# A Mamba block with an FP4-quantised feed-forward: the two silu visits of a chunk each split into two halves

## What is computed

```python
h = layernorm(x) * (1 + ca) + sa
xc, z = split(h @ W_in.T)                 # 1024 channels each
xc = silu(causal_conv(xc))                # four taps per channel
dlt, B, C = split(xc @ W_xproj.T)         # 32, 16, 16 columns
delta = softplus(dlt @ W_dt.T + b_dt)
# for each channel d and each of 16 states n, over time t:
s[t] = exp(delta * A)[t] * s[t-1] + (delta * B * xc)[t]
y[t] = sum_n s[t, d, n] * C[t, n] + D * xc
x = x + ga * ((y * silu(z)) @ W_out.T)
x = x + gb * ffn(layernorm(x) * (1 + cb) + sb)   # three fp4-quantised linears
```

## Time and profile before

| | |
|---|---|
| median of 3 runs | 5216.49 us (5215.18 to 5220.55) |
| the profiled execution | 5215.41 us, span 5213.5 us |
| mean granted TensorE clock | 0.979 of full speed |
| busy share of the span | PE 91%, DVE 91%, POOL 73%, ACT 66% |
| first scan to first scan of the next chunk | 214.9 to 215.4 us in the chunks after the first |

### The profile page before, as it was taken

The page is one execution under the profiler, slowest core; times in us unless marked ns, Lnnn a source line. Parts: engine busy times, 40 slices in busy tenths (PEclk is TensorE's granted clock), DMA queues, the critical chain, the costliest instruction groups (busy, mean ns, idle before and its releaser), DMA issues. The chain is left out here.

```text
span 5213.5 us, 65887 instructions
## 1 busy us (share of the span) xinstructions
PE 4746.8 (91%) x21964; PEld 3282.5 (63%) x21964; DVE 4731.3 (91%) x3781; ACT 3466.9 (66%) x7501; POOL 3807.4 (73%) x1770
## 2 busy tenths in 40 slices
PE   8789899898988988989889898877999999999999
PEld 3455555555555555555555555555888888888888
DVE  7899999999999999999999999997888888888887
ACT  3787878778787787877877778765444444444442
...
GB/s 252 173 188 191 190 198 184 195 191 187 201 183 193 195 186 201 182 192 196 187 203 184 192 193 182 192 174 156 25 33 35 31 31 37 31 31 37 31 31 29
DMA packets 402664, 745.70 MB, mean 143 GB/s; under 512 B 44083, under 2 KB 44211, under 8 KB 402198
## 3 DMA queue, kind: packets, MB, share of 16 engines
...
...
## 5 line engine op out<-in xcount | busy, mean ns | idle before, releaser
L725 POOL TENSOR_TENSOR slot<-du,b_row 128x1024 f32<-128x1024 f32 x1024 | 2395.7, 2367 | 2.2 <-DMA down_quantised<-slot 1.2
L1070 DVE TENSOR_TENSOR_SCAN decays<-decays,state,slot 128x1024 f32<-128x1024 f32 x704 | 1650.2, 2344 | 43.8 <-ACT slot L944 42.7
L935 ACT ACTIVATE decays<-delta,rate 128x512 f32<-128x512 f32 x2048 | 1328.5, 681 | 24.4 <-issue 0.2
L1203 PEld LDWEIGHTS y_ps<-ident,slot 128*128 128x128 f32 x8192 | 957.6, 144 | 307.0 <-issue 246.2
L1126 PE MATMUL work_ps<-h_t,win 128*128 128x512 f32 x2048 | 958.5, 612 | 158.1 <-ACT delta L859 109.1
L1203 PE MATMUL y_ps<-ident,slot 128*128 128x128 f32 x8192 | 1039.0, 277 | 38.6 <-POOL slot L732 26.9
L1076 DVE TENSOR_TENSOR slot<-decays,c_row 128x1024 f32<-128x1024 f32 x704 | 861.7, 1224 | 68.6 <-DVE decays L1070 2.3
L1588 POOL TENSOR_TENSOR hq<-hid,qinv 128x1408 f32<-128x1408 f32 x63 | 163.4, 2593 | 1018.5 <-DVE qinv L1614 1018.5
L732 POOL TENSOR_TENSOR slot<-slot,c_row 128x1024 f32<-128x1024 f32 x320 | 755.1, 2360 | 147.6 <-ACT state L921 145.6
L1070 DVE TENSOR_TENSOR_SCAN slot<-decays,state,slot 128x1024 f32<-128x1024 f32 x320 | 749.9, 2343 | 47.1 <-ACT slot L944 47.1
L1126 PEld LDWEIGHTS work_ps<-h_t,win 128*128 128x128 f32 x2048 | 382.0, 195 | 586.2 <-issue 468.0
...
## 6 DMA issues: line engine op xcount, KB each, us to landing
b_row<-b_c_rows SPq DMA_DIRECT2D x1024, 256.0 KB, 3.9
c_row<-b_c_rows SPq DMA_DIRECT2D x1024, 256.0 KB, 3.7
...
```

Source lines behind the costliest of these rows:

```text
L725: pool.tensor_tensor(slot[:, u % SLOTS, :, :], du[:, p % 2, :, :], two(b_row[:, u % BC_RING, :]), ALU.mult).then_inc(S["ub_ready"], 1)
L935: act.activation(decay[u % 2][:, i, :], delta[:, p % 2, i, :], ACT.Exp, scale=rate[:, 2 * p + i, n:n + 1]).then_inc(S["decay_ready"], 1)
L1070: dve.tensor_tensor_scan(d if u in DVE_C else h, d, h, state[:, 2 * p, n:n + 1], ALU.mult, ALU.add).then_inc(S["scan_done"], 1)
L1203: op = pe.matmul(y_ps[i][:, s, :], slot[:, u % SLOTS, i, s * P:(s + 1) * P], ident[:, :], is_transpose=True, start=False, stop=(n == N - 1 ...
```

## The change

Each silu piece gets an argument h of 0 or 1 and works on four channel blocks (128 x 2048), with a table load before and after it as the whole one had. `silu_z` stands in units 11 and 21, `silu_x` in units 45 and 53. The semaphores of the two count two per chunk: a gate of blocks 0 to 3 waits for the first half alone; `x`, `du` and `xd` wait for both halves of xc.

All tables are written anew. Unit 8 and unit 19 are now in `DVE_C` and unit 9 is not; unit 48 takes the place of unit 47. So 45 units instead of 44 have their product with C on DVE. Four of the 49 bank numbers differ. The core of the diff:

```diff
 BANK = {
-    ("c", 7): 1, ("i", 1): 0, ("o", 2): 1, ("y", 3): 0,
+    ("c", 7): 0, ("i", 1): 1, ("o", 2): 0, ("y", 3): 1,
...
 ACT_STEPS = {
-    20: [("residual", 2, -1)], 21: [("silu_z", 0, 0)],
-    53: [("silu_x", 0, 1)], 54: [("z_out", 0, 1)],
+    10: [("z_out", 6, 0), ("residual", 0, -1)], 11: [("silu_z", 0, 0)],
+    20: [("residual", 2, -1), ("ln_apply", 2, 1), ("y_out", 1, 0)],
+    21: [("silu_z", 1, 0)], 22: [("ln_apply", 3, 1)],
+    45: [("in_out", 6, 1), ("silu_x", 0, 1)], 53: [("silu_x", 1, 1)],
...
 DVE_STEPS = {
-    (4, 0): [("gate", 6, -1)], (4, 1): [("gate", 7, -1)], (21, 0): [("gate", 0, 0)], (52, 1): [("gate", 5, 0)],
+    (4, 1): [("gate", 6, -1), ("gate", 7, -1)], (20, 1): [("gate", 0, 0)], (52, 0): [("gate", 5, 0)],
...
-                    def silu_z(_, c):
-                        for ka in last_pieces("z").values():
-                            wait(act, *piece_read(*ka, c))
-                        act.activation(zs[:, :, :], zs[:, :, :], ACT.Silu).then_inc(S["zs_ready"], 1)
+                    def silu_z(h, c):
+                        part = range(h * NB // 2, (h + 1) * NB // 2)
+                        for j in {BANK["z", j]: j for j in part}.values():
+                            wait(act, *piece_read("z", j, c))
+                        v = zs[:, part.start:part.stop, :]
+                        act.activation(v, v, ACT.Silu).then_inc(S["zs_ready"], 1)
                         act.preload_act_table_set("natural_log_exp_and_others")
...
-                        wait(dve, S["zs_ready"], c.at(1, 1))
+                        wait(dve, S["zs_ready"], c.at(2, j // (NB // 2) + 1))
...
-                        wait(pe, S["xc_ready"], c.at(1, 1))
+                        wait(pe, S["xc_ready"], c.at(2, 2))
```

More of the change, by code:

```diff
@@ L60 @@
[L60 to L64, removed]
@@ L65 @@
-    34: [("conv_out", 1, 1), ("y_out", 3, 0), ("y_out", 2, 0), ("xd", 4, 0)], 36: [("in_out", 3, 1)],
-    37: [("conv_out", 2, 1), ("xd", 7, 0)], 38: [("in_out", 4, 1)], 39: [("softplus", 3, 0)],
-    41: [("conv_out", 3, 1), ("xd", 6, 0)], 43: [("conv_out", 4, 1)], 44: [("lead", 3, 0), ("in_out", 5, 1)],
-    45: [("in_out", 6, 1)], 46: [("conv_out", 5, 1)], 48: [("conv_out", 6, 1)], 49: [("in_out", 7, 1)],
-    50: [("conv_out", 7, 1)], 51: [("y_out", 5, 0), ("y_out", 4, 0)], 53: [("silu_x", 0, 1)], 54: [("z_out", 0, 1)],
@@ L70 @@
-    56: [("x_out", 0, 1)], 57: [("softplus", 0, 1)], 58: [("xd", 0, 1)], 61: [("z_out", 1, 1), ("ln_sum", 0, 2)],
-    62: [("z_out", 2, 1), ("lead", 0, 1)], 63: [("z_out", 3, 1)],
+    0: [("ln_sum", 1, 1), ("xd", 0, 0), ("z_out", 4, 0)], 2: [("y_out", 6, -1)], 3: [("softplus", 1, 0)],
+    4: [("ln_sum", 2, 1), ("y_out", 7, -1)], 5: [("z_out", 5, 0), ("ln_sum", 3, 1), ("ln_square", 0, 1)],
+    6: [("ln_square", 1, 1), ("ln_square", 2, 1)], 7: [("ln_square", 3, 1), ("xd", 3, 0)],
+    9: [("seed", 0, 1), ("lead", 1, 0)], 10: [("z_out", 6, 0), ("residual", 0, -1)], 11: [("silu_z", 0, 0)],
@@ new lines @@
+    14: [("z_out", 7, 0), ("xd", 2, 0)], 15: [("residual", 1, -1), ("ln_apply", 0, 1)], 16: [("softplus", 2, 0)],
+    19: [("ln_apply", 1, 1), ("y_out", 0, 0)], 20: [("residual", 2, -1), ("ln_apply", 2, 1), ("y_out", 1, 0)],
+    21: [("silu_z", 1, 0)], 22: [("ln_apply", 3, 1)], 23: [("h_out", 2, 1)], 24: [("residual", 3, -1)],
+    25: [("h_out", 0, 1), ("lead", 2, 0), ("h_out", 3, 1), ("h_out", 1, 1)], 27: [("in_out", 0, 1)],
+    28: [("in_out", 1, 1)], 29: [("xd", 5, 0)], 31: [("in_out", 2, 1), ("conv_out", 0, 1)], 32: [("xd", 4, 0)],
@@ new lines @@
+    33: [("conv_out", 1, 1)], 34: [("y_out", 2, 0)], 35: [("y_out", 3, 0)], 36: [("in_out", 3, 1)],
+    37: [("xd", 7, 0), ("conv_out", 2, 1)], 38: [("in_out", 4, 1)], 39: [("softplus", 3, 0)],
+    42: [("xd", 6, 0), ("conv_out", 3, 1)], 43: [("conv_out", 4, 1)], 44: [("lead", 3, 0), ("in_out", 5, 1)],
+    45: [("in_out", 6, 1), ("silu_x", 0, 1)], 46: [("conv_out", 5, 1)], 48: [("in_out", 7, 1)],
+    49: [("conv_out", 6, 1)], 50: [("conv_out", 7, 1)], 51: [("y_out", 5, 0), ("y_out", 4, 0)], 53: [("silu_x", 1, 1)],
@@ L72 @@
+    55: [("z_out", 0, 1)], 56: [("x_out", 0, 1)], 57: [("softplus", 0, 1)], 60: [("ln_sum", 0, 2)],
+    61: [("z_out", 1, 1), ("lead", 0, 1)], 62: [("z_out", 2, 1)], 63: [("z_out", 3, 1), ("xd", 1, 1)],
 }
 DVE_STEPS = {
-    (4, 0): [("gate", 6, -1)], (4, 1): [("gate", 7, -1)], (21, 0): [("gate", 0, 0)], (33, 0): [("gate", 1, 0)],
-    (37, 0): [("gate", 2, 0)], (50, 0): [("gate", 3, 0)], (51, 1): [("gate", 4, 0)], (52, 1): [("gate", 5, 0)],
+    (4, 1): [("gate", 6, -1), ("gate", 7, -1)], (20, 1): [("gate", 0, 0)], (33, 0): [("gate", 1, 0)],
@@ L76 @@
+    (36, 1): [("gate", 2, 0)], (49, 0): [("gate", 3, 0)], (51, 1): [("gate", 4, 0)], (52, 0): [("gate", 5, 0)],
     (55, 1): [("x_low", 0, 1)],
@@ L658, in du_of @@
                     def du_of(p, c):
-                        wait(pool, S["xc_ready"], c.at(1, 1))
+                        wait(pool, S["xc_ready"], c.at(2, 2))
                         for j in (2 * p, 2 * p + 1):
@@ L825, in z_out, with silu_x @@
                         act.activation(zs[:, j, :], work_ps[b][:, :], ACT.Copy).then_inc(bank_free[b], 1)
-                    def silu_x(_, c):
-                        for ka in last_pieces("c").values():
-                            wait(act, *piece_read(*ka, c))
+                    def silu_x(h, c):
+                        part = range(h * NB // 2, (h + 1) * NB // 2)
+                        for j in {BANK["c", j]: j for j in part}.values():
+                            wait(act, *piece_read("c", j, c))
                         if c.reg is None and c.off == 0:
@@ L880, in skip_out @@
                     def skip_out(j, c):
-                        wait(act, S["xc_ready"], c.at(1, 1))
+                        wait(act, S["xc_ready"], c.at(2, 2))
                         wait(act, S["sum_done"], c.at(UNITS, N * (j // 2 - 1) + 1))
```

32 lines of the change are left out of this document (15 added, 17 removed), and 30 rows, old and new, of tables (BANK, PE_STEPS).

## The result

The changed kernel takes **5264.52 us** (median of 4 runs, 5262.28 to 5266.84); the kernel before took 5216.41 us beside it (5215.18 to 5220.55). The ratio is 1.0094, with a 95% interval of 1.0082 to 1.0106. It is slower by 48 us, 0.9%, where no change was forecast, and it lies above the range. The profiled execution has a span of 5260.5 us and a mean granted TensorE clock of 0.973 (0.979 before).

What follows compares the result with a forecast made beforehand. DVE, with ACT one step ahead, was taken to set the chunk: 1.2 us less waiting and 1.5 more work make 0.3 us more, times 15.5 chunks 5 us, so 5220 us (no change). The range was 5183 to 5248 us.

Steps and rivals of the forecast that it cites:

- A half leaves 0.9 us uncovered, the split gains at most 0.8 per visit by itself.: ACT's half visit: 4.5 us long, 0.9 us uncovered for DVE at best; a whole visit leaves 2.6.
- New wait 2.2: DVE before scan 46, behind the first half of silu_x in unit 45: a new wait of 2.2 us.
- The sum of waits: DVE's waits per chunk, scan to scan: 5.6 us (1.6 + 0.7 + 0.4 + 0.7 + 2.2) in place of 6.8.
- the five places of the forecast: DVE's remaining waits: 1.6 at unit 12, 0.7 at 17, 0.4 at 22, 0.7 at 29 and 40, 2.2 at 46.
- Gate 6 ... its y is there: 0.6 gone.: DVE's gate 6 moves 1.14 us later, behind unit 4's product, so its 0.6 us wait for the transposed y goes.
- PE has slack there, since ACT waited for it in that stretch before.: Behind the half visit in unit 45, PE's wait for evictions of c and i pieces was held harmless.
- the second rival: PE comes late: 2 us a chunk of stalls reach DVE through ACT's evictions; 5251 us, chance 0.27.
- It decides from 0.4 us a chunk on: Threshold for PE's stalls reaching DVE to make the kernel slower: 0.4 us a chunk.
- One more unit with its product: 1.33: DVE's added work from one more product with C: 3.59 - 2.26 = 1.33 us a chunk.
- 0.2 for the gates: DVE's gates 6 and 0 leave the scan-product gap, 5 enters it: 0.2 us a chunk net, an estimate.
- The loads aren't hidden: Rival: every added ACT table load lengthens the chunk, 4 x 1.28 = 5.1 us a chunk, 5294 us; chance 0.03.
- forecast 0.3: Net chunk growth: 1.2 us less waiting, 1.5 us more DVE work, so 0.3 us more a chunk.

Runs made afterwards that it cites:

- warm_c3: The changed kernel with 14 transposes of zeros on PE in unit 38, in the wait ahead of piece c 3; 5243.2 us, ratio 1.0055.
- x_split: The kernel before with its old tables and only silu_x split, halves in units 45 and 53; 5249.8 us, ratio 1.0067.
- before_late_c3: The kernel before with 33 transposes of zeros on PE in unit 38 ahead of piece c 3, making it late; 5239.3 us, ratio 1.0054.
- products_44: The changed kernel with the kernel before's list of 44 products with C on DVE; 5267.1 us, ratio 1.0106.
- warm_both: The changed kernel with 14 transposes of zeros on PE ahead of c 3 and 30 ahead of z 5; 5268.4 us, ratio 1.0104.
- before_warm: The kernel before with 30 transposes of zeros on PE ahead of piece z 5; 5216.5 us, ratio 1.0006.
- c6_back: The changed kernel with convolution piece c 6 back in PE's unit 43 instead of 42; 5255.0 us, ratio 1.0079.

## Why the prediction was wrong

Point by point, by its own steps:

- **"A half leaves 0.9 us uncovered, the split gains at most 0.8 per visit by itself."** Held in size, though no run shows the 0.8 as a gain: visit and return 4.52 us, ACTIVATE 1.91, 1.24 behind the half that started nearly on time. What the places add was as foreseen at 12 (1.66 for 1.5), 22 (0.35 for 0.3) and 54 (none).
- **"New wait 2.2" at unit 46**: 2.56, and 1.93 where c 3 is at full clock. The size without PE's lateness was right.
- **The sum of waits.** In warm_c3 the five places of the forecast (12, 17, 22, 29 and 40, 46) wait 1.55 + 0.50 + 0.34 + 0.88 + 1.93 = 5.2 us, which is the forecast's sum in the same measure. Missing were waits that it put at nothing: units 0 and 4, the gates and unit 50, 0.18 + 0.23 + 0.38 + 0.27 = 1.1 us.
- **"Gate 6 ... its y is there: 0.6 gone."** Wrong. Gate 6 moved 1.14 us back, but z 5, which stands ahead of its transpose on PE, takes 6.5 to 6.7 us instead of 5.37, and gate 7 waits too.
- **"PE has slack there, since ACT waited for it in that stretch before."** This is the step that failed, and it read the row the wrong way round. An engine that others wait for is the late one. PE is busy 27.93 of 28.00 us from c 3 on. In x_split the half visit alone makes PE wait 2.54 us there, and units 50 to 52 of DVE then wait 1.54. In before_late_c3 1.63 us of lateness, without any visit added, make the chunk 1.70 longer (with z 5's share in it). I had read PE's idle time (21.8 us a chunk) as if it lay everywhere. With it goes a term that the sum put at nothing without a reason, PE's granted clock: its fall at c 3 is worth 1.69 us a chunk by warm_c3. Without that fall the time, 5243.2 us, lies inside the range.
- **"Should 2 us a chunk of such stalls reach ACT's evictions ... 5251 us"**, the second rival. It is what happened, in kind. The stall was not one of those that I named (sums behind `y_out`, a bank of `z_out`) but PE's clock behind a wait that both kernels have, 1.7 us a chunk. Its chance of 0.27 was too low. "It decides from 0.4 us a chunk on" fits.
- **"One more unit with its product: 1.33"** and 0.2 for the gates: DVE's work grew by 1.5 to 1.8 us, so the size holds. But products_44 shows that going back to the old 44 gives nothing: the products cover waits of the same size.
- **The loads aren't hidden**, 5.1 us a chunk: no. In warm_c3 the whole excess over the kernel before is 1.7 us a chunk, with all four loads in it.

Together: forecast 0.3, the fall at c 3 1.7 and the small waits 1.1 make 3.1 of the measured growth of the chunk, 3.4 (218.43 - 215.01). The 0.3 left over is in waits just above and below the bracket's limit and in rounding; it isn't the work on DVE, which in warm_c3 is 1.5 us above before, as forecast. Times 15.5 the 3.4 is 53 us, for 48 measured: the first two chunks grew by 0.7 us together, not by 6.8. The 1.7 is shown by warm_c3, which takes it out; before_late_c3 puts PE's lateness in and finds a growth of the same size, of which some belongs to z 5. The 1.1 of small waits is read from the trace and was not taken out by itself; warm_both, meant for it, met a new fall.

**Open**: why the clock falls at c 3 in the changed kernel and not in the one before, behind the same wait of 1.82 us. In the 10 us ahead of that wait's end PE was busy 7.83 us in the one and 8.18 in the other:

```profile
1569.70:1579.70 10.00, 7.83 (x40) 4.85 (x38) 9.79 (x7) 7.98 (x19) 9.90 (x5) 1.00 0.40 135
```

(the row of before reads 10.00, 8.18), since a wait of 0.36 us stands in that stretch that the kernel before doesn't have. In before_warm and c6_back the clock at the same piece falls in some chunks and not in others, so small shifts seem to decide it. Which of them, no run here tells.
